# Each value product of an attention written as two products of 64 stationary columns, on the two column halves of TensorE's array

## The reference

```python
q = ln @ Wq.T
kv = jnp.concatenate([xn @ Wkv.T, ln @ Wlkv.T], axis=1)   # 64 context rows and 1024 tokens
...
attn = jnp.einsum('bhid,bhjd->bhij', qn, kn)              # scores of 1024 queries and 1088 keys
attn = jnp.where(full_mask[:, None, None, :], attn, -jnp.finfo(attn.dtype).max)
attn = jax.nn.softmax(attn, axis=-1)
out = jnp.einsum('bhij,bhjd->bhid', attn, v)              # the value products
out = out.transpose(0, 2, 1, 3).reshape(b, m, INNER)
return out @ Wo.T + bo
```

## Time and profile before

| | |
|---|---|
| median of 3 runs | 1053.68 us (1052.32 to 1054.23) |
| profiled execution, its own time | 1053.49 us |
| its span in the trace | 1051.9 us |
| instructions in the trace | 19167 |
| TensorE (PE) busy | 957.8 us, 91% of the span |
| TensorE's weight loads (PEld) busy | 749.0 us, 71% |
| VectorE (DVE) busy | 578.6 us, 55% |
| ScalarE (ACT) busy | 475.5 us, 45% |
| GpSimd (POOL) busy | 319.6 us, 30% |
| mean granted clock of TensorE | 0.951 of full speed |

### The profile page before, as it was taken

How to read it: one execution, slowest core, us unless ns; L and a number is a source line. 1 busy time by engine, 2 the same in 40 slices (tenths; PEclk the granted TensorE clock), 3 DMA queues, 4 the chain that set the end, 5 groups by cost and what they waited for, 6 DMA issues and landing times. The chain is left out here.

```text
span 1051.9 us, 19167 instructions
## 1 busy us (share of the span) xinstructions
PE 957.8 (91%) x5932; PEld 749.0 (71%) x5932; DVE 578.6 (55%) x1562; ACT 475.5 (45%) x909; POOL 319.6 (30%) x279
## 2 busy tenths in 40 slices
PE   4899999999999999999986059999999999999991
PEld 4555556665566655656445059999999999999991
DVE  5545455646656464562534525767666757756660
ACT  3645643445444454444421124644544446535440
POOL 3421311213542135321050613424242324232321
PEclk8999999999999999998996579999999999999996
DMA  4100100101101011110021542435252524352325
GB/s 120 43 1 1 43 1 1 41 1 42 48 34 40 1 63 64 36 41 1 6 76 40 151 126 40 121 54 135 40 130 45 134 41 113 62 131 44 45 35 169
DMA packets 45049, 62.07 MB, mean 59 GB/s; under 512 B 7344, under 2 KB 38832, under 8 KB 44944
## 3 DMA queue, kind: packets, MB, share of 16 engines
q0 software_dynamic: 17520, 33.27, 14.4%
q1 hardware_dynamic: 25136, 25.98, 8.3%
q10 hardware_dynamic: 2352, 2.31, 0.8%
HBM read 37.34 MB, written 28.39 MB: 62 GB/s over the span
## 5 line engine op out<-in xcount | busy, mean ns | idle before, releaser
L1218 PE MATMUL psO<-p_ring,V 128*128 128x512 f32 x576 | 267.7, 596 | 0.8 <-ACT o_sb L622 0.8
L633 ACT ACTIVATE p_ring<-psS,shift 128x1024 f32<-128x1024 f32 x128 | 136.8, 1111 | 165.9 <-PE psS L1203 165.9
L1535 PE MATMUL psH<-xT_hi,Q 128*128 128x256 f32 x1120 | 203.7, 281 | 1.6 <-DVE xT_lo L1452 1.6
L1548 PE MATMUL psY<-K,g_hi 128*128 128x256 f32 x1120 | 203.4, 284 | 0.0
L1388 POOL DMA_INDIRECT total<-y_out,token_i x70 | 116.3, 1661 | 252.7 <-DVE y_out L1473 240.0
L1535 PEld LDWEIGHTS psH<-xT_hi,Q 128*128 128x128 f32 x1120 | 174.4, 189 | 2.0 <-issue 2.0
L475 POOL TENSOR_TENSOR rr<-ssm,minus_half 128x4 f32<-128x4 f32 (+1 forms) x72 | 70.3, 977 | 346.1 <-DVE ssm L741 346.0
L1548 PEld LDWEIGHTS psY<-K,g_hi 128*128 128x128 f32 x1120 | 171.7, 189 | 0.0
L1218 PEld LDWEIGHTS psO<-p_ring,V 128*128 128x128 f32 x576 | 105.1, 190 | 91.6 <-issue 90.5
L1548 PE MATMUL psY<-K,g_lo 128*128 128x256 f32 x560 | 157.3, 281 | 0.0
L1535 PE MATMUL psH<-xT_lo,Q 128*128 128x256 f32 x560 | 157.2, 281 | 0.0
(11 more groups left out here) (224 smaller groups left out, 1174.7 us busy)
## 6 DMA issues: line engine op xcount, KB each, us to landing
lnf<-routed SPq DMA_DIRECT2D x35, 258.0 KB
xr<-in_L_ffn_w POOLq DMA_DIRECT2D x7, 1024.0 KB, 6.3
xn<-in_L_ffn_w POOLq DMA_DIRECT2D x7, 1024.0 KB, 8.7
xr<-in_x SPq DMA_DIRECT2D x8, 512.0 KB, 4.6
total<-xb SPq DMA_DIRECT2D x4, 1024.0 KB, 4.5
routed<-pad_rows SPq DMA_DIRECT2D x8, 258.0 KB, 4.2
total<-y_out,token_i POOLq DMA_INDIRECT x70, 3.9
routed<-big,slot_i POOLq DMA_INDIRECT x64, 2.6
```

The lines of the kernel that those rows point to most:

```text
L633: act.activation(p_ring[0:p, u % RING, :], psS[u % 2][0:p].rearrange("p a n -> p (a n)"), ACT.Exp, bias=bias).then_inc(exp_done, 1)
L1218: ins = pe.matmul(psO[odd][:], V[:, (w % 2) * KT + kt, odd * DH:odd * DH + P], p_ring[:, u % RING, odd * HALF:(odd + 1) * HALF], start=(kt ...
L1535: ins = pe.matmul(o, l, r, start=(n == 0), stop=(n == len(parts) - 1))
L1548: ins = pe.matmul(psY[m][:, 0:D], l[:, c, cols], r[:, c, :], start=(c == 0 and n == 0), stop=(c == HC - 1 and n == 2))
```

## The change

Each value product is issued as two. The first has columns 0 to 63 of the former stationary matrix and writes partitions 0 to 63 of `psO[odd]`; the second has columns 64 to 127 and writes partitions 64 to 127. Each has all 128 rows and the same 512 moving columns of `p_ring`. The first is placed on the left half of the array's columns and the second on the right half. The loop over the two heads and the semaphore behind the last product stay.

```diff
-                        ins = pe.matmul(psO[odd][:], V[:, (w % 2) * KT + kt, odd * DH:odd * DH + P],
-                                        p_ring[:, u % RING, odd * HALF:(odd + 1) * HALF], start=(kt == 0), stop=(kt == KT - 1))
+                        for part in range(2):
+                            ins = pe.matmul(psO[odd][part * DH:(part + 1) * DH, :],
+                                            V[:, (w % 2) * KT + kt, (odd + part) * DH:(odd + part + 1) * DH],
+                                            p_ring[:, u % RING, odd * HALF:(odd + 1) * HALF], start=(kt == 0), stop=(kt == KT - 1))
```

## The result

| | |
|---|---|
| after | 1076.74 us, median of 4 runs (1074.85 to 1080.38) |
| before, beside it | 1053.0 us, median of 4 runs (1051.52 to 1054.23) |
| ratio | 1.023, 95% interval 1.0199 to 1.0262: slower by 23.7 us |
| profiled execution after | 1076.13 us, span 1074.3 us, mean granted clock 0.956 |

The sign and the place are as forecast; the size is not. 75.8 us were forecast, 23.7 came, and the time lies under the range of 1080 to 1190. It is near the rival without a stagger (1081 us), which had a chance of 4%.

The account below looks back on a forecast made before the run. TensorE was taken to bound the attention; the profiled 1053.5 us plus 47.9 for the stagger and 27.9 for changes of shape, other terms 0, gave 1129 us, range 1080 to 1190 us.

Parts of the forecast that it names:

- rival without a stagger: Matmuls of a pair don't keep the assumed order, so only the changes of shape cost: 1081 us; chance 4%.
- What bounds the kernel: TensorE, busy 497.5 of 500 us in the attention, has no slack there; what the change costs it, the kernel pays.
- Step 1: Value matmuls double from 576 to 1152, each with all 512 moving columns and still 0.428 us long.
- Serial halves: In the value products, the second half's matmul waits until the first half's is through: 1328 us; chance 16%.
- Step 2, the stagger: Halves overlap, but starts keep written order, so each of 112 uninterrupted value rows takes one slot more: 47.9 us.
- Step 3: New changes of array shape around the values, 94 entries at 0.21 us and 51 exits at 0.16: 27.9 us.
- Step 4: Weight loads of at most 0.19 us fit beside the value matmuls: 0, or 11 us if they stretch them.
- exposed loads: A half's weights load only once the matmul ahead has started, two bare loads per product: 1184 to 1238 us; chance 10%.
- Step 5: ScalarE and VectorE have half their time free in the attention, so later value results add 0.

Follow-up runs that it names:

- narrow_right: Changed kernel with the right half given only 128 of the 512 moving columns, except in the first key tile; 1080.36 us in one run.
- left_first: Changed kernel issuing both left products of a unit first, then both right ones; 1081.82 us, ratio 1.0258.
- heads_paired: Changed kernel with a unit's products reordered: first head's V and second head's V side by side, then the ones; 1079.09 us, ratio 1.024.
- split_again: Changed kernel run once more without alteration; 1077.21 us, ratio 1.0226.
- split_held: Changed kernel with the third sequence's 16 indirect DMAs held until the attention's last results are taken; 1081.47 us, ratio 1.0261.
- quarters_late: The quarters kernel with the last 8 of the third sequence's 16 indirect DMAs held until the last values are taken; 1024.49 us, ratio 0.9761.
- moving_halves: Kernel before with each value product split into two of 256 moving columns on the full array; 1056.76 us, ratio 1.0064.
- whole_together: Kernel before with the tile's steps and other uses put ahead of both units' values; 1106.98 us, ratio 1.0506.
- quarters: Version of the changed kernel with V as two 32-column products and the ones as two with half the moving columns each; 1035.31 us, ratio 0.9832.

## Why the prediction was wrong in size

**What bounds the kernel** was right: all that was lost was lost on TensorE in the attention, and the experts' stretch is 438.2 us against 437.9.

**Step 1** was right. The slot is 0.428 us with half the stationary columns too, and the two halves work at once. Serial halves (16%) are refuted.

**Step 2, the stagger, failed, and it is the step that makes the prediction wrong.** Its 47.9 us (112 rows of one slot) are 0. It took for granted that matmuls start in the order in which they stand: "Right 1 stands behind left 2, so it starts with it, not with left 1." They do so only within a half. narrow_right shows it outright, left_first and heads_paired by units of four slots. The scores, from which I had taken that halves work at once, could not have told me: there the order alternates between the halves.

**Step 3** had the right mechanism and a size too large: 27.9 us forecast, 20.1 to 20.9 measured. 145 changes at 20.4 are 0.14 us each, where I had set 0.21 for the 94 entries and 0.16 for the exits. The trace of after gives 0.14 for an entry (0.09 us later behind L1103 or the transposes, and 0.05 more from the first value matmul to the next) and 0.15 for an exit into transposes (0.09 and 0.06), 0.20 into the products L1103. That makes 13.3 + 8.2 = 21.5 us. I had overlooked a small gain: the 17 entries from work of 64 rows, mostly the scores, became 0.05 us shorter each, which takes off 0.9 and leaves 20.6. The prices had been taken from the change of rows.

**Step 4** was right: loads cost nothing, so exposed loads (10%) are refuted, and the 11 us set above them are 0.

**Step 5** was not right at the end of the attention. "0" has to read 8.1 us there, for a stall of ScalarE and then of TensorE beside GpSimd's DMAs. In the execution of after the clock gave back 5.2; in split_again it gave back nothing, and 4.0 us came back behind the attention.

With steps 1 to 4 as measured it would have been 1053.5 + 20.4 = 1074 us, and with the stall, less what was given back, 1053.5 + 20.4 + 8.1 - 5.2 = 1076.8; it was 1076.1 in the profiled execution. The rival without a stagger gave 1081 with the larger step 3: two errors of opposite sign, 7.5 too much and the stall's rest too little.

**What stays open** is what holds ScalarE and TensorE in the stall. The DMAs must lie beside it (split_held, quarters_late), halves needn't (moving_halves, whole_together), and the kernel before, with the same DMAs at the same distance (its scores 12.8 us behind the first of them, 12.6 after), hasn't got it. I looked for late loads of instructions: among the DMA packets of after, none of that kind lies between 543.3 and 581, which speaks against an instruction that arrived late. Neither the count of TensorE's instructions nor that distance sorts the cases. Also open is where the rest of what quarters should have brought has gone.

## What to carry to other kernels

Before counting a stagger between parts of the array, ask what the order of starts is bound to: in this kernel it was bound within a part only, and the written order of the parts didn't matter. Splitting a product by columns gained nothing here while each half still had to take as many moving columns as the whole had, and cost about 0.15 us wherever it touched work of the full array; it paid when the parts let me drop work that was there only to fill the array, such as half of the ones here. And a stretch whose sum fits to the microsecond can still have its last group twice as long: look at the ends of a stage, beside a burst of DMAs, on their own.

## What the runs showed of the hardware that I had not expected

- The column halves go on independently of each other, as far as the runs reach: a right half's matmul started while three of the four left ones ahead of it had not, and narrow ones ran ahead into the next head's product. The Trainium skill, page "TensorEngine Tiling (Array Packing)", section "Key Properties", says that tiles operate independently; that is what all of these runs show, and taken at its word it speaks against the stagger. Its page "TensorE: Matmul & The Clock Gate", section "The mechanism", note on what overlaps, says that matmuls keep the order of the program in start and end, and that a weight load overlaps matmuls in flight only where the row group differs. Neither holds here: in narrow_right four narrow matmuls had started by 260.1 against one wide, and loads for two halves on the same rows lay beside running matmuls (251.65, 0.14 us) and cost nothing.
- A change between the full array and column halves costs 0.14 us in and 0.15 us out into transposes (0.20 into products), where that between row shapes costs 0.16 and 0.21.
- Plain float32 products run on quarters of 32 columns at the same 0.428 us for 512 moving columns, all of them at once (quarters_late).
- ScalarE can stand still for 8.6 us with its input written (552.74 to 561.36), in a stretch in which GpSimd issues an indirect DMA each 1.28 us.
